# Ring of three tiles up to quad 60, sums for quads 73 to 76, and the change into block 1 by halves

## The chip, the cores and the metric

The kernel runs on one core of one Trainium2 chip. The metric is the device time of one execution in microseconds (us), lower is better. TensorE (PE) multiplies matrices, ScalarE (ACT) applies functions, VectorE (DVE) does elementwise work and reductions, GpSimd (POOL) small elementwise work, SyncE (SP) issues DMAs.

## What is computed

Attention with an additive score over 77 context tokens, and then an FFN with weights and activations rounded to FP4 by blocks of 16. The rows are 2 x 2048 with 512 features.

```
x = x + _L0_xattn_ref(_layernorm(x), mask, ctx, mask2, Ws, W, w, b, Wcw, bcw, Wcb, bcb)
x = x + _L0_ffn_ref(_layernorm(x), w_gate, w_up, w_down)

def _L0_xattn_ref(features, masks, textual_features, q_masks, Ws, W, w, b, Wcw, bcw, Wcb, bcb):
    txt_proj = einsum('btd,de->bte', textual_features, Ws)
    feat_proj = einsum('bfd,de->bfe', features, W)
    h = tanh(txt_proj[:, None, :, :] + feat_proj[:, :, None, :] + b)
    rho = einsum('bftd,d->bft', h, w[:, 0]) + (1.0 - q_masks)[:, None, :] * NEG
    att = softmax(rho, axis=-1)
    txt_h = einsum('bft,btd->bfd', att, textual_features)
    w_s = tanh(einsum('bfd,od->bfo', txt_h, Wcw) + bcw)
    b_s = tanh(einsum('bfd,od->bfo', txt_h, Wcb) + bcb)
    return w_s * features + b_s

def _L0_ffn_ref(x, w_gate, w_up, w_down):          # fp4_linear rounds x and w to FP4
    h = silu(fp4_linear(x, w_gate)) * fp4_linear(x, w_up)
    return fp4_linear(h, w_down)
```

## The kernel before

**Tanh and scores.** The 4096 rows are four blocks of 1024. For each block, tanh is taken of (features + text) for 77 tokens x 512 features. The work is cut into quads, 77 a block (QPB), numbered through all blocks: quad n is four rows of 1024 columns (128 features x 1024 rows of x, for four pairs of token and feature group). ACT makes a quad with four ACTIVATEs, features plus a bias column a token, into a place of a ring (`tanh_quad`, L628). PE scores it with 8 products of 512 columns into `rho` (`score_quad`, L809) and frees the place. Some quads are summed: DVE adds the bias column first (`sum_quad`, L985), into a room (`room_of`), and ACT then needs one ACTIVATE of 4096 columns (L623). `ring_pos` says which place a quad uses and `ring_prev` which quad it must wait for. In block 0 the ring has the two places of `hring` and a third, `HEAD_PLACE`: 4 is a part of `featT` that later blocks' features fill, 3 is `wd_room`, which the down weights fill later, None is no third place. Before: place 4 for quads up to 42, none for 43 and 44, place 3 for 45 to 60. The eight quads `FIRST_SUMS` are summed in `wd_room`, in the rounds `SUM_ROUNDS` of DVE.

**The head, block 0.** Beside the quads, PE turns and projects the rows of blocks 1 to 3 in twelve pairs of tiles: `turn_pair(w)` (L824) waits for `pair_normal` of GpSimd (L501) and writes the banks tr and dn, DVE copies them (`copy_pair`, L1120), PE projects (`project_pair`, L836, two halves), DVE copies the features out (`features_pair`, L1131). Pair w is tied to quad 8 + 9w/2. A DVE round w is: `copy_pair(w)`, a sum, `gate_up_weights(w + 1)` (rounding weights to FP4, with the statistics of two pairs in every other round), `features_pair(w - 1)`, a sum. Then DVE rounds the down weights, which SP transposes into `wd_room` after the last quad that used it (`LAST_IN_WD`).

**The change into block 1.** After quad 76, DVE adds the mask (`softmax_drain`, L1219), PE transposes the scores, DVE subtracts the maxima (`softmax_shift`), ACT takes the exponentials of both halves (L636), DVE makes the sums `garg` for both halves (`softmax_sums`), ACT takes the tanh `gates` (L655), DVE makes the factors and then tile 0 of the FFN (`rows_tile(0)`), which SP transposes for PE. ACT meanwhile makes the quads of block 1, of which PE scores seven (`PRE_QUADS`) before FFN tile 0.

**The stream.** From then on PE walks through 32 FFN tiles t of 7 pieces p: four gate and up pieces (L892) and three down pieces of the tile before (L906). `slots[t, p]` says how many quads it scores behind each piece, spread by the costs `G_COST` and `D_COST` between the ends of two blocks; `before[t, n]` counts quads up to a piece. ACT makes quads up to `before[t, n]` plus the ring's depth, then the silu of a piece (L661). DVE multiplies (`hidden`, L1309), rounds (`quantise_hidden`) and sums quads in between. Block k ends in tile `BASE[k] - 2`, that is 6, 14 and 22, `SOFTMAX_AT`, with its softmax there. The last quads stand in tile 22. Each engine runs its list in order and waits on semaphores.

## Time and profile before

| | us |
|---|---|
| median of 3 timed runs | 1537.94 |
| lowest, highest | 1537.92, 1540.9 |
| the profiled execution, its own time | 1539.24 |
| its span in the profile | 1537.4 |
| PE busy | 1432.1 (93%) |
| ACT busy | 1359.6 (88%) |
| DVE busy | 1157.2 (75%) |
| POOL busy | 248.7 (16%) |

Start times below are from the span's start. A row of the order of time gives the start of a group of like instructions, how long it lasts, engine and line, output and input tiles with sizes, how many (x), and in brackets how long the engine stood idle before it and what it waited for. "issue" there is a wait without a releaser in the profile. Two ACTIVATEs overlap by a little, so the difference of two starts is the cost of one.

### The profile page before, as it was taken

To read this page: it belongs to the slowest core of one execution; us is meant where nothing else is said; L and a number is where in the kernel's file an instruction comes from. 1 tells how busy PE (TensorE), PEld (TensorE's weight loads), DVE (VectorE), ACT (ScalarE), POOL (GpSimd) and SP (SyncE) were. 2 spreads that over 40 slices of the span, in tenths; PEclk is the share of its full clock that TensorE was granted. 3 is DMA by queue.
4 is the path that set the end of the run, shared out by engine and by line. 5 is a ranking of instruction groups with operands and counts; after the bars stand their busy time and mean duration, and the time that the engine had idled before them with its cause. 6 is when DMAs were issued, how large, how long until landed. Compare 5 with 4: busy or idle time off the path is not lost.

```text
span 1537.4 us, 24122 instructions
## 1 busy us (share of the span) xinstructions
PE 1432.1 (93%) x9752; PEld 647.7 (42%) x9752; DVE 1157.2 (75%) x1783; ACT 1359.6 (88%) x1249; POOL 248.7 (16%) x389
## 2 busy tenths in 40 slices
PE   7988889856999999999999999989999999999998
PEld 4444444411333333334444444434444444555564
DVE  4699997944586666759666776698877787898887
ACT  5999989999999999999999999999999999433321
POOL 0122222200111010111011111011101111312211
PEclk9999999988999999999999999999999999999999
DMA  5133332320011111201111111112111111123332
GB/s 159 42 83 83 83 82 75 95 65 8 8 26 41 40 27 41 40 15 40 41 40 40 41 33 37 36 40 40 40 41 41 40 41 40 40 59 73 80 69 62
DMA packets 181557, 77.91 MB, mean 51 GB/s; under 512 B 163627, under 2 KB 165675, under 8 KB 181445
## 3 DMA queue, kind: packets, MB, share of 16 engines
q1 hardware_dynamic: 180224, 75.00, 21.0%
q8 instruction: 76, 1.25, 0.3%
q10 hardware_dynamic: 1221, 1.36, 0.3%
q14 instruction: 36, 0.29, 0.1%
HBM read 27.85 MB, written 8.39 MB: 24 GB/s over the span
## 4 chain that ended last, share of the span: by engine, by line
PE 52%; ACT 27%; DVE 17%; issue 2%; DMA 1%; POOL 1%; SPq 0%; ACTq 0%; DVEq 0%; POOLq 0%
PE rho L809 19%; ACT hring L628 17%; PE dn L906 10%; PE gu1g L892 5%; PE gu0g L892 5%; PE gu1u L892 5%; PE gu0u L892 5%; ACT hring L623 4%; DVE featT L985 2%; ACT wd_room L628 2%; DVE work L1019 2%; ACT featT L623 1%; ACT featT L628 1%; DVE work L1040 1%; DVE work L1039 1%
## 5 line engine op out<-in xcount | busy, mean ns | idle before, releaser
L628 ACT ACTIVATE hring<-featT,bias 128x1024 f32<-128x1024 f32 x688 | 729.2, 1156 | 2.6 <-PE rho L809 2.5
L809 PE MATMUL rho<-hring,wslide 128*32 128x512 f32 x3776 | 459.0, 611 | 61.5 <-ACT hring L628 52.4
L809 PEld LDWEIGHTS rho<-hring,wslide 128*32 128x32 f32 x3776 | 105.5, 111 | 338.6 <-issue 191.7
L628 ACT ACTIVATE featT<-featT,bias 128x1024 f32<-128x1024 f32 x220 | 236.3, 1178 | 2.2 <-PE rho L809 2.2
L906 PE MATMUL dn<-wd_room,turned 128*128 128x512 f16 x1023 | 230.6, 380 | 0.2 <-DMA turned<-work 0.2
L490 POOL TENSOR_SCALAR split_t<-sm 128x32 f32<-128x32 f32 (+4 forms) x82 | 19.7, 240 | 1178.1 <-DVE sm L1008 1178.1
L623 ACT ACTIVATE hring<-featT 128x4096 f32<-128x4096 f32 x57 | 207.5, 3640 | 0.4 <-DVE featT L985 0.4
L985 DVE TENSOR_SCALAR featT<-featT,bias 128x1024 f32<-128x1024 f32 x256 | 175.5, 750 | 11.9 <-ACT hring L623 7.6
L1309 DVE TENSOR_TENSOR work<-sg,gu1u 128x352 f32<-128x352 f32 x64 | 33.3, 521 | 173.9 <-ACT sg L661 173.1
L906 PEld LDWEIGHTS dn<-wd_room,turned 128*128 128x128 f16 x1023 | 96.4, 98 | 145.2 <-issue 36.0
L809 PE MATMUL rho<-featT,wslide 128*32 128x512 f32 x1056 | 126.4, 596 | 5.4 <-ACT featT L628 3.1
L892 PE MATMUL gu1g<-wgu,turned 128*128 128x352 f16 x768 | 125.5, 313 | 4.1 <-DVE work L1309 3.9
L892 PE MATMUL gu0g<-wgu,turned 128*128 128x352 f16 x768 | 125.5, 313 | 2.3 <-DVE work L1309 1.9
L892 PE MATMUL gu0u<-wgu,turned 128*128 128x352 f16 x768 | 125.0, 313 | 0.0
L892 PE MATMUL gu1u<-wgu,turned 128*128 128x352 f16 x768 | 125.0, 313 | 0.0
L493 POOL TENSOR_TENSOR s_lo<-sm,s_hi 128x32 f16<-128x32 f32 (+4 forms) x82 | 111.0, 1353 | 6.4
L892 PEld LDWEIGHTS gu1g<-wgu,turned 128*128 128x128 f16 x768 | 71.8, 98 | 72.5 <-issue 28.5
L892 PEld LDWEIGHTS gu0g<-wgu,turned 128*128 128x128 f16 x768 | 71.8, 98 | 72.4 <-issue 26.8
L892 PEld LDWEIGHTS gu0u<-wgu,turned 128*128 128x128 f16 x768 | 75.1, 98 | 39.4
L892 PEld LDWEIGHTS gu1u<-wgu,turned 128*128 128x128 f16 x768 | 75.2, 98 | 39.3
L661 ACT ACTIVATE sg<-gu1g 128x352 f32<-128x352 f32 x64 | 30.5, 476 | 60.4 <-PE gu1u L892 60.4
L661 ACT ACTIVATE sg<-gu0g 128x352 f32<-128x352 f32 x64 | 30.5, 477 | 52.6 <-PE gu0u L892 52.5
(228 smaller groups left out, 1578.5 us busy)
## 6 DMA issues: line engine op xcount, KB each, us to landing
xt<-in_x SPq DMA_DIRECT2D x32, 256.0 KB, 2.8
out<-xt SPq DMA_DIRECT2D x32, 256.0 KB, 2.3
work<-in_x SPq DMA_DIRECT2D x8, 512.0 KB, 4.1
xt<-in_x SPq DMA_DIRECT2D x6, 512.0 KB, 4.3
xt<-in_L_ffn_w_gate SPq DMA_DIRECT2D x11, 256.0 KB, 2.7
xt<-in_L_ffn_w_up SPq DMA_DIRECT2D x11, 256.0 KB, 3.0
work<-in_L_ffn_w_down SPq DMA_DIRECT2D x2, 704.0 KB, 5.1
xt<-in_L_ffn_w_down SPq DMA_DIRECT2D x2, 704.0 KB, 4.1
```

Source lines behind the costliest of these rows:

```text
L490: small(pool.tensor_scalar(t, s, SPLIT, 1.0, ALU.mult, ALU.mult))
L493: pool.tensor_tensor(s_lo[:, 0:nb], s, s_hi[:, 0:nb], ALU.subtract).then_inc(split_ready, 1)
L623: act.activation(slot[s], rooms[room_of[n]], ACT.Tanh).then_inc(tanh_ready, GRP)
L628: act.activation(slot[s][:, g, :], featT[:, e, ROW0[k]:ROW0[k] + rows], ACT.Tanh, bias=bias[:, e, base + tok:base + tok + 1]).then_inc(tan ...
L661: act.activation(sg[:, n % 2, :], gu[n % 2][0][:, 0:GU_N], ACT.Silu, scale=1.0 / W_PRE).then_inc(sg_ready, 1)
L809: last = pe.matmul(rho[SLOTW * g:SLOTW * g + SLOTW, hf * 512:hf * 512 + 512], wslide[:, e, SLOTW - 1 - r:2 * SLOTW - 1 - r], slot[s][:, g, ...
L892: last = pe.matmul(ps[:, 0:GU_N], xqT[:, a, k, :], w[:, bb, k, n * GU_N:n * GU_N + GU_N], start=(k == 0 and i == 0), stop=(k == KC - 1 and ...
L906: last = pe.matmul(dn[:, :], hqT[:, a, c, :], wd[:, bb, c, :], start=(c == 0 and i == 0), stop=(c == NC - 1 and i == 2))
L985: dve.tensor_scalar(rooms[room_of[n]][:, g, :], featT[:, e, ROW0[k]:ROW0[k] + BLOCKS[k]], bias[:, e, tok:tok + 1], None, ALU.add).then_inc ...
L1019: ins = tt(a.rearrange("p (i q b) -> p i b q", **natural), src.rearrange("p (i b q) -> p i b q", **natural), r.rearrange("p (i b) -> p i b ...
L1039: step(tt(a, a, big, ALU.add))
L1309: signal(tt(h, sg[:, n % 2, :], gu[n % 2][1][:, 0:GU_N], ALU.mult), gu_drained[n % 2], 2 * t + n // 2 + 1)
```

## The change

- `PRE_QUADS` is 5 instead of 7.
- The third place in block 0 is place 4 up to quad 51 and place 3 for quads 52 to 60.
- A ninth first sum, quad 49, in DVE round 8. Four late sums, quads 73 to 76: 73 and 75 in a room of two pieces (`stage` and part of `turned`, two ACTIVATEs of 2048 columns), 74 and 76 in `work`. DVE makes the first behind the last down weights and the others behind the wait for their transposing; 75 waits for the tanh of 73, 76 for that of 74.
- Block 1 has 23 summed quads instead of 22, from its quad 7 on (before from 12).
- For even pairs w > 0, PE now does both halves of `project_pair(w - 1)` one quad earlier and `turn_pair(w)` behind them.
- The sums, gates and factors of the change into block 1 are made by halves of four tiles: half 0, tile 0, half 1.
- Block 1 ends in tile 6 after piece 4 instead of 2, and block 2 starts accordingly. DVE puts block 1's drain and shifts into the rounding of tile 6 and the sums behind it. ACT makes quads up to 156 before the exponentials.

```diff
-PRE_QUADS = 7
+PRE_QUADS = 5
-    HEAD_PLACE = [4] * 43 + [None] * 2 + [3] * 16 + [None] * (QPB - 61)
-    SUM_ROUNDS = (0, 2, 4, 6)
-    FIRST_SUMS = (13, 17, 22, 26, 31, 35, 40, 44)
+    HEAD_PLACE = [4] * 52 + [3] * 9 + [None] * (QPB - 61)
+    SUM_ROUNDS = (0, 2, 4, 6, 8)
+    FIRST_SUMS = (13, 17, 22, 26, 31, 35, 40, 44, 49)
+    LATE_SUMS = (73, 74, 75, 76)
...
+    ENDS = [(0, -1), (BASE[1] - 2, 4), *((b - 2, 2) for b in BASE[2:])]
...
-    SUMS = {1: range(12, QPB, 3), 2: [3, *range(11, QPB, 4)], 3: [2, 5, *range(11, QPB, 3)]}
+    WHOLE = {1: range(7, QPB - 3, 3), 2: [3, *range(11, QPB, 4)], 3: [2, 5, *range(11, QPB, 3)]}
...
@@ scalar, change into block 1 @@
             tanh_quad(issued, range(3, 4))
-            tanh_quad(issued + 1)
-            tanh_quad(issued + 2, range(0, 1))
-            softmax_gates(0)
-            tanh_quad(issued + 2, range(1, 4))
-            issued += 3
+            tanh_quad(issued + 1, range(0, 2))
+            half_gates(0, first_garg, first_gates)
+            tanh_quad(issued + 1, range(2, 4))
+            tanh_quad(issued + 2)
+            tanh_quad(issued + 3)
+            half_gates(1, garg_ready, gates_ready)
+            issued += 4
@@ scalar, SOFTMAX_AT @@
-                    if issued < QUADS:
+                    goal = 2 * QPB + 3 if SOFTMAX_AT[t] == 1 else min(issued + 1, QUADS)
+                    while issued < goal:
@@ tensor, quads of block 0 @@
                     at = 8 + 9 * w // 2
-                    if n == at and w < PAIRS:
+                    behind = w % 2 == 0 and w > 0
+                    if n == at and w < PAIRS and not behind:
                         turn_pair(w)
-                    if n == at + 1 and w > 0:
+                    if n == at + (0 if behind else 1) and w > 0:
                         project_pair(w - 1, 0)
-                    if n == at + 2 and w > 0:
+                    if n == at + (1 if behind else 2) and w > 0:
                         project_pair(w - 1, 1)
+                        if behind and w < PAIRS:
+                            turn_pair(w)
@@ vector, rounds @@
-                if w in SUM_ROUNDS:
+                if w in SUM_ROUNDS[:-1]:
                     sum_quad()
...
             down_weights(3)
+            sum_quad()
             dve.wait_ge(wd_turned, 16 * KC)
+            for _ in LATE_SUMS[1:]:
+                sum_quad()
@@ vector, new @@
+            def first_sums(hf, made):
+                part = slice(4 * hf, 4 * hf + 4)
+                e = rhoS[:, hf * 512:hf * 512 + 512].rearrange("p (t s) -> p t s", t=4)[:, :, 0:TOK]
+                t = prod.rearrange("p (t s) -> p t s", t=4)[:, :, 0:TOK]
+                dve.wait_ge(exp_ready, hf + 1)
+                step(dve.tensor_reduce(den[:, part], e, axis=AX_X, op=ALU.add))
+                step(dve.reciprocal(den[:, part], den[:, part]))
+                for u in range(2):
+                    step(tt(t, e, uv[:, 0, u, :].unsqueeze(1).broadcast_to([P, 4, TOK]), ALU.mult))
+                    step(dve.tensor_reduce(garg[:, u, part], t, axis=AX_X, op=ALU.add))
+                    ins = tt(garg[:, u, part], garg[:, u, part], den[:, part], ALU.mult)
...
+            def first_factors(hf, made):
...
+                dve.wait_ge(made, 2)
...
@@ vector, change into block 1 @@
-            softmax_sums(0)
-            softmax_factors(0)
+            first_sums(0, first_garg)
+            first_factors(0, first_gates)
             rows_tile(0)
+            first_sums(1, garg_ready)
+            first_factors(1, gates_ready)
+            first_results(1)
+            sum_quads(QPB + 4)
@@ vector, tile 6 @@
+                if begun == 1:
+                    rows_tile(t + 1)
+                    hidden(t, 2)
+                    hidden(t, 3)
...
+                    quantise_hidden(t, between=lambda: softmax_drain(1), midway=shifts)
+                    softmax_sums(1)
```

PE in block 0, from quads 15 and 16 on, before. `rho<-` rows are scores (x8 is a quad), `gu1g` and `gu1u` are the halves of `project_pair(1)`, `tr` and `dn` from `work` are `turn_pair(2)`:

```order
42 L809 MATMUL rho<-hring,wslide 32x512 x16
43 L809 MATMUL rho<-featT,wslide 32x512 x8
44 L824 MATMUL tr<-idf,work 128x128 x4
45 L824 MATMUL dn<-idf,work 128x128 x4
46 L809 MATMUL rho<-hring,wslide 32x512 x8
47 L836 MATMUL gu1g<-stage,turned 128x256 x8
48 L809 MATMUL rho<-hring,wslide 32x512 x8
49 L836 MATMUL gu1u<-stage,turned 128x256 x8
50 L809 MATMUL rho<-featT,wslide 32x512 x8
```

The same place now:

```order
42 L834 MATMUL rho<-hring,wslide 32x512 x16
43 L834 MATMUL rho<-featT,wslide 32x512 x8
44 L861 MATMUL gu1g<-stage,turned 128x256 x8
45 L834 MATMUL rho<-hring,wslide 32x512 x8
46 L861 MATMUL gu1u<-stage,turned 128x256 x8
47 L849 MATMUL tr<-idf,work 128x128 x4
48 L849 MATMUL dn<-idf,work 128x128 x4
49 L834 MATMUL rho<-hring,wslide 32x512 x8
50 L834 MATMUL rho<-featT,wslide 32x512 x8
```

The turning of pair 2 moved from behind quad 17 to behind both projection halves and quad 18.

ACT at the end of block 0, before (a row of 128x1024 is a fourth of a quad, `stage<-stage` are the exponentials, `sg` is the first silu of the stream):

```order
64 L628 ACTIVATE hring<-featT,bias 128x1024 x71
65 L636 ACTIVATE stage<-stage 128x4x77 x2
66 L628 ACTIVATE hring<-featT,bias 128x1024 x6
67 L655 ACTIVATE gates<-garg,bc 128x8 x2
68 L628 ACTIVATE hring<-featT,bias 128x1024 x23
69 L661 ACT_TABLE_LOAD
70 L661 ACTIVATE sg<-gu0g 128x352
```

And now:

```order
65 L638 ACTIVATE hring<-stage 128x2048
66 L638 ACTIVATE hring<-turned 128x2048
67 L638 ACTIVATE hring<-work 128x4096
68 L638 ACTIVATE hring<-stage 128x2048
69 L638 ACTIVATE hring<-turned 128x2048
70 L638 ACTIVATE hring<-work 128x4096
71 L644 ACTIVATE hring<-featT,bias 128x1024 x7
72 L652 ACTIVATE stage<-stage 128x4x77 x2
73 L644 ACTIVATE hring<-featT,bias 128x1024 x3
74 L711 ACTIVATE gates<-garg,bc 128x4 x2
75 L644 ACTIVATE hring<-featT,bias 128x1024 x10
76 L711 ACTIVATE gates<-garg,bc 128x4 x2
```

Quads 73 to 76 come from rooms, the gates stand in two pairs, and the second pair stands ten rows behind the first.

DVE at the change into block 1, before (the end of the sums of half 1, then the factors):

```order
378 L1252 TENSOR_REDUCE garg<-stage 128x4
379 L1253 TENSOR_TENSOR garg<-garg,den 128x4
380 L1251 TENSOR_TENSOR stage<-stage,uv 128x4x77
381 L1252 TENSOR_REDUCE garg<-stage 128x4
382 L1253 TENSOR_TENSOR garg<-garg,den 128x4
383 L1266 TENSOR_TENSOR beta<-gates,rstd 128x8
```

And now, from the end of tile 0's rounding:

```order
410 L1075 TENSOR_TENSOR xq<-work,s_lo 128x512
411 L1339 TENSOR_TENSOR beta<-beta,stat 128x4
412 L1340 TENSOR_TENSOR beta<-gates,beta 128x4
413 L1374 TENSOR_SCALAR xt<-xt,alpha,beta 128x512
414 L1312 TENSOR_REDUCE den<-stage 128x4
415 L1313 RECIPROCAL den<-den 128x4
416 L1315 TENSOR_TENSOR stage<-stage,uv 128x4x77
417 L1316 TENSOR_REDUCE garg<-stage 128x4
```

The sums of half 1 moved from ahead of the factors to behind tile 0.

## Rows read from the trace of the kernel before

**Rows 1.** Windows: busy PE, PEld, DVE, ACT, POOL (instructions), granted clock, DMA, GB/s

```profile
77.00:227.00 150.00, 132.51 (x872) 68.63 (x868) 143.14 (x231) 143.21 (x119) 40.45 (x48) 0.97 0.31 79
308.00:357.00 49.00, 29.71 (x204) 7.37 (x200) 20.74 (x23) 48.78 (x47) 3.63 (x4) 0.84 0.22 52
390.00:1314.00 924.00, 891.70 (x6423) 370.91 (x6420) 674.85 (x990) 920.77 (x798) 124.49 (x180) 1.00 0.17 36
```

**Rows 2.** Order of time, ACT in block 0: summed quads and waits

```profile
153.50 3.62 ACT L623 ACTIVATE hring<-wd_room 128x4096 f32<-128x4096 f32 x1 [0.40 <-DVE wd_room L985]
158.27 4.27 ACT L628 ACTIVATE featT<-featT,bias 128x1024 f32<-128x1024 f32 x4 [1.15 <-PE rho L809]
...
170.76 3.60 ACT L623 ACTIVATE featT<-wd_room 128x4096 f32<-128x4096 f32 x1
174.26 8.42 ACT L628 ACTIVATE hring<-featT,bias 128x1024 f32<-128x1024 f32 x8
...
192.03 3.62 ACT L623 ACTIVATE hring<-wd_room 128x4096 f32<-128x4096 f32 x1 [1.04 <-DVE wd_room L985]
196.67 4.27 ACT L628 ACTIVATE featT<-featT,bias 128x1024 f32<-128x1024 f32 x4 [1.02 <-PE rho L809]
...
212.32 3.62 ACT L623 ACTIVATE hring<-wd_room 128x4096 f32<-128x4096 f32 x1 [3.07 <-issue]
...
308.22 48.95 ACT L628 ACTIVATE hring<-featT,bias 128x1024 f32<-128x1024 f32 x47 [0.58 <-PE rho L809]
```

**Rows 3.** Order of time, PE around the turning of pair 2

```profile
100.39 1.92 PE L809 MATMUL rho<-featT,wslide 128*32 128x512 f32 x16 [0.37 <-ACT featT L623]
104.03 0.66 PE L824 MATMUL tr<-idf,work 128*128 128x128 f32 x4 [1.71 <-POOL work L501]
...
105.05 1.92 PE L809 MATMUL rho<-hring,wslide 128*32 128x512 f32 x16
106.90 3.72 PE L836 MATMUL gu1g<-stage,turned 128*128 128x256 f32 x16
110.55 1.92 PE L809 MATMUL rho<-hring,wslide 128*32 128x512 f32 x16
```

**Rows 4.** Order of time, DVE: copies of pairs 2 and 8, a sum, a wait

```profile
110.60 0.69 DVE L1120 COPY stage<-tr 128x512 f32<-128x512 f32 x1
...
189.17 2.74 DVE L985 TENSOR_SCALAR wd_room<-featT,bias 128x1024 f32<-128x1024 f32 x4
...
226.32 0.69 DVE L1120 COPY stage<-tr 128x512 f32<-128x512 f32 x1
...
268.98 0.69 DVE L1131 COPY featT<-gu1g 128x512 f32<-128x512 f32 x1 [8.17 <-PE gu1u L836]
```

**Rows 5.** Order of time, DVE and then ACT, the change into block 1

```profile
351.94 1.29 DVE L1219 TENSOR_SCALAR stage<-rho,negm 128x1024 f32<-128x1024 f32 x1 [20.45 <-PE rho L809]
...
360.79 0.47 DVE L1247 TENSOR_REDUCE den<-stage 128x4 f32<-128x308 f32 x1
...
364.71 0.17 DVE L1266 TENSOR_TENSOR beta<-gates,rstd 128x8 f32<-128x8 f32 x1 [0.79 <-ACT gates L655]
...
374.95 0.55 DVE L1303 TENSOR_SCALAR xt<-xt,alpha,beta 128x512 f32<-128x512 f32 x1
...
357.07 0.80 ACT L636 ACTIVATE stage<-stage 128x308 f32<-128x308 f32 x2
...
364.13 0.47 ACT L655 ACTIVATE gates<-garg,bc 128x8 f32<-128x8 f32 x2
364.51 23.99 ACT L628 ACTIVATE hring<-featT,bias 128x1024 f32<-128x1024 f32 x23
```

**Rows 6.** Order of time, block 1's softmax in tile 6: DVE, then ACT

```profile
698.57 0.17 DVE L1253 TENSOR_TENSOR garg<-garg,den 128x4 f32<-128x4 f32 x1
...
700.53 0.47 ACT L655 ACTIVATE gates<-garg,bc 128x8 f32<-128x8 f32 x2
```

**Rows 7.** Order of time, ACT: the last scores are drained

```profile
1316.33 1.11 ACT L640 ACTIVATE stage<-rho,negm 128x1024 f32<-128x1024 f32 x1 [1.70 <-PE rho L809]
```

91 lines of the change are left out of this document (66 added, 25 removed).

## The prediction

> **What bounds the kernel now.** Three views, in this order. The busy time by stretch [rows 1]: between 390 and 1314 us ScalarE (ACT) is busy for 920.77 of 924.00 us, TensorE (PE) for 891.70, VectorE (DVE) for 674.85. The reader is to see that ACT, which makes the tanh tiles that PE scores, has 3.2 us of room in the whole stretch. So whatever lets ACT enter it earlier, or takes work from it there, moves the end one for one, as long as PE and DVE keep up. The last scores are drained at 1316.33 [rows 7]; what follows is FFN work that the change leaves alone, so the tail keeps its length.
> The second view is ACT's order of time in block 0 [rows 2]. It waits six times between 150 and 310 us: 0.40 and 1.04 us for a sum by DVE, and 1.15, 1.02, 3.07 and 0.58 us for a ring place (the 3.07 us carries no releaser; quad 44 goes there into the place of quad 42). In the same region DVE is busy 143.14 of 150.00 us in 231 instructions [rows 1], with some 0.03 us between two of them: it never stands still, and what delays DVE there delays every later sum. The third view is the order of time around the change into block 1 [rows 5].
>
> The unit is read from ACT's rows. The 47 rows from 308.22 to the exponentials at 357.07 are quads 67 to 77 and three rows of quad 78 [rows 2, 5]: 48.85 / 47 = 1.039 us a row, 4.16 us a quad. A summed quad takes 174.26 - 170.76 = 3.50 us [rows 2], so a sum saves ACT 0.65 us. Quad 76 ends at 308.22 + 40 x 1.039 = 349.8; I call this E.
>
> **Part 1, the order of PE in the head.** For even pairs turn_pair now stands behind both halves of project_pair. For pair 2 before, PE took quad 17 at 100.39, waited 1.71 us for GpSimd, and turned from 104.03 to 105.05 [rows 3]. Now: quad 17 takes 1.86 us, to 102.25; a half projection takes 110.55 - 106.90 = 3.65 us, to 105.9; quad 18 to 107.8; the second half to 111.4; the turning, 1.02 us, to 112.45. DVE wanted the result at 110.60 [rows 4]. It now waits 1.9 us, and as it has no idle time, its chain of rounds runs 1.9 us later from there. For pairs 4 and 6 the same steps put the end of the turning at 148.7 and 187.2; DVE wants them at 151.1 and 189.6 with its delay, so 2.4 us are left and nothing is added. Behind DVE's wait stand the sums for quads 22 to 44, and ACT waits for those.
> ACT then runs so. Quad 31: its sum comes 1.9 us later than before, and it starts at 155.4 instead of 153.50. Quad 32: its wait of 1.15 us is gone, since PE no longer holds scores back behind GpSimd: 0.75 us late. Quad 40: ACT arrives at 192.03 - 1.04 + 0.75 = 191.7, the sum (189.17 + 2.74 + 1.9 [rows 4]) is there at 193.8: again 1.9 late. Quad 41: its 1.02 us is gone: 0.9 us late.
>
> **Part 2, three ring places up to quad 60.** Quad 44 goes to the third place, free since quad 41 is scored, so the 3.07 us goes: it starts at 196.67 + 0.9 + 3 x 4.16 = 210.05 instead of 212.32. What is late next is the new ninth sum, for quad 49: DVE copies pair 8 from 226.32 + 1.9 on (two copies of 0.69 us), then sums for 2.74 us, ready at 232.4 [rows 4]. ACT would be there at 210.05 + 3.50 + 4 x 4.16 = 230.2 and starts at 232.5; before, it was there at 232.7. So nearly all that the third place gives is spent waiting: 0.2 us is left, and 0.65 us by the sum itself. The sum's own 2.74 us on DVE is hidden, since DVE idled 8.17 us at 269 [rows 4]. From quad 61 on the ring has two places while the last pair is projected: two waits of about 0.5 us where there was one of 0.58, 0.4 us lost. At quad 67: **-0.45 us**.
>
> **Part 3, late sums for quads 73 to 76.** Two, in one piece of 4096 columns, save 0.65 us each. The other two come in two pieces of 2048. No row shows such a piece; between 1024 columns at 1.04 us and 4096 at 3.50 us a straight line gives 1.86, two of them 3.72, a saving of 0.43. The bounds for a quad are 4.16 and 3.50. In sum -2.2 us (bounds -1.3 and -2.6). The Trainium skill (ScalarE: Activation LUTs, What ACT_TABLE_LOAD costs) gives 186 ns + 0.833 ns a column, less 93 ns of overlap, without a bias pointer; by it two pieces would take 3.60 us and the sum would be 0.2 us better. By that rule 4096 columns take 3.50 us, and the trace agrees. The cover: sums 75 and 76 can only start when the tanh of 73 and 74 has emptied their room, and need 2.74 us against the 3.5 to 3.7 us of the quad between: 0.8 us to spare. DVE itself is free, it waited 20.45 us for the last scores [rows 5]. E becomes 349.8 - 0.45 - 2.2 = 347.2: **-2.6 us**.
>
> **Part 4, the change into block 1 by halves.** Half 0 is what PE's tile 0 needs, and it comes earlier: its gates stand 3 rows behind the exponentials instead of 6. But ACT's own order now asks for the gates of half 1 ten rows after those of half 0, 10.4 us. Between them DVE has to make the factors, tile 0, the betas and the row's result (364.71 to 374.95 + 0.55, 10.8 us), then the sums of half 1 (360.79 to 364.71 - 0.79, 3.1 us) [rows 5]: 13.9 us, with signals 14.15. **ACT waits 3.75 us** for garg. This wait did not exist, since the sums of both halves stood ahead of the gates. Behind it on ACT stand quads 82 and on, the whole stretch that has no room. Two more gate instructions cost 364.51 - 364.13 = 0.38 us. PE can start tile 0 some 12 us earlier than before, but then it waits for tanh tiles; its own work is not what bounds. In sum **+4.1 us**. GpSimd's share of tile 0 and SP's transposing keep their order.
>
> **Part 5, the stream.** One more sum in block 1: -0.65 us. PRE_QUADS 5 puts the same quads two earlier against the tiles; ACT's list is as long as before. Block 1's end moves two pieces on in tile 6. Before, garg was there at 698.57 + 0.16, 1.8 us ahead of ACT's gates at 700.53 [rows 6]. Now DVE ends the quantising first. From the end of quad 153's tanh ACT has three quads, the table and exponentials (2.1), a summed quad and a quad: 22.3 us. DVE has PE's score (1.9), the drain (1.3), a sum (2.7), two steps and both shifts with PE between them (5), the rest of the quantising (5.1) and twice 3.1 for garg: 22.3 us too. I take no wait (bounds 0 and 2.7, should one sum more fall ahead of garg).
>
> **Sum:** -2.6 + 4.1 - 0.65 = +0.85 us. On the profiled execution's 1539.24 us that is 1540.1; that execution lies 1.3 us above the median of the three timed runs, 1537.94. I forecast the median: **1538.8 us**. A measurement of this kernel can tell about 0.2% (3.1 us) from no change; this is within it.
>
> **Rivals.**
> R1, slower: DVE slips again. The decisive place is turn_pair of pairs 4 and 6, with 2.4 us to spare. Should PE run a half projection there at 1.2 GHz (the granted clock was 0.97 in the mean of 77 to 227 us, so for a part of it at the lower level [rows 1]), it takes 3.65 us more, the reserve is gone, and two slips of about 2 us reach quads 40 and 49: +4.9, 1542.8. For it: the same happens at pair 2 by my count. Against it: PE's waits for GpSimd, behind which it was slow, are what the new order removes.
> R2, faster: the wait at the second gates is small and DVE does not slip at pair 2. Then 3.75 and 1.9 us come off at most: -4.8, 1533.1. Against it: both are sums of rows on engines that have nothing else to do.
> R3: PE is at the lower clock (mean 0.84 between 308 and 357 us [rows 1]) when it scores quad 76; that takes 1.8 us more, DVE's chain to the exponentials is 0.4 us ahead of ACT, and ACT waits 1.4: +2.3, 1540.2. The Trainium skill (TensorE: Matmul & The Clock Gate, HAM oscillation) says that idle gaps put the array back to half speed; by it the two quads fewer ahead of tile 0 would make this likelier.
> R4: the stream's 3.2 us of waits [rows 1] go: -2.3, 1535.6; or tile 6 costs its 2.7: 1541.5.
> R5: the change doesn't do what it says, the late sums come late and save nothing: +3.05, 1541.0.
>
> **How the numbers follow.** Forecast as summed, 0.50, its own range 1537.3 to 1540.4; R1 0.15; R2 0.13; R3 0.07; R4 0.07; R5 0.08. Faster by over 3.1 us is R2: 0.13. Slower by over 3.1 us is R1, half of R5 and 0.01 of the forecast's tail: 0.20. Within: 0.67. The range 1535.0 to 1543.0 leaves out R2 and the outer part of R1, under 2 in 10.
>
> **What would show it.** Right: ACT waits 3 to 4.5 us before the second pair of gates and 2 to 2.5 us before quads 31, 40 and 49, for DVE's sums; it has no wait at quads 32, 41 and 44; DVE waits about 2 us for the turned pair 2; E is near 347. Wrong: under 1 us at the second gates, or ACT busy under 915 of 924 us in the stream, which would mean that PE or DVE has become what bounds.

## The result and the profile after

| | before | after |
|---|---|---|
| median | 1538.24 us (8 runs) | 1543.86 us (8 runs) |
| lowest, highest | 1537.81, 1540.9 | 1541.2, 1545.79 |
| ratio, 95% interval | | 1.0032 [1.0022, 1.0041] |
| the profiled execution | 1539.24 us | 1541.2 us |

The change makes the kernel 4.9 us slower (0.0032 of 1538). The forecast was 1538.8 us, in a range of 1535.0 to 1543.0; the measured median lies above it. The profiled execution after is the lowest of its eight. The same kernel, measured again in the run e1_again below (profiled at 1543.47 us), is nearer to the median, so the ledger has both.

The windows of the kernel after, which answer to [rows 1]: PE, PEld, DVE, ACT and POOL busy, granted clock, DMA, GB/s.

```profile
77.00:227.00 150.00, 136.95 (x904) 71.41 (x896) 141.28 (x229) 145.92 (x122) 42.36 (x48) 0.97 0.31 79
308.00:357.00 49.00, 30.51 (x212) 7.33 (x208) 31.96 (x45) 48.42 (x41) 3.67 (x4) 0.86 0.22 52
390.00:1314.00 924.00, 888.73 (x6392) 369.92 (x6394) 669.24 (x981) 919.00 (x795) 124.47 (x180) 1.00 0.17 36
```

ACT now stands still for 5.0 us of the 924 instead of 3.2, although it is still the engine that bounds. Where it stands, the order of time shows. ACT in block 0, answering to [rows 2]; "<-" names what ended the wait:

```profile
153.96 3.62 ACT L638 ACTIVATE hring<-wd_room 128x4096 f32<-128x4096 f32 x1 [1.99 <-DVE wd_room L1015]
...
192.28 3.62 ACT L638 ACTIVATE hring<-wd_room 128x4096 f32<-128x4096 f32 x1 [2.09 <-PE rho L834]
...
208.28 3.60 ACT L638 ACTIVATE featT<-wd_room 128x4096 f32<-128x4096 f32 x1
...
230.61 3.62 ACT L638 ACTIVATE hring<-wd_room 128x4096 f32<-128x4096 f32 x1 [2.10 <-PE rho L834]
...
284.71 16.74 ACT L644 ACTIVATE hring<-featT,bias 128x1024 f32<-128x1024 f32 x16 [0.58 <-PE rho L834]
...
302.03 29.22 ACT L644 ACTIVATE hring<-featT,bias 128x1024 f32<-128x1024 f32 x28 [0.58 <-PE rho L834]
...
338.94 1.93 ACT L638 ACTIVATE hring<-stage 128x2048 f32<-128x2048 f32 x1 [0.58 <-PE rho L834]
340.77 1.89 ACT L638 ACTIVATE hring<-turned 128x2048 f32<-128x2048 f32 x1
342.57 3.60 ACT L638 ACTIVATE hring<-work 128x4096 f32<-128x4096 f32 x1
```

Quads 31, 40 and 49 wait 2.0 to 2.1 us each; quad 44 (208.28) waits for nothing. At 192.28 and 230.61 the row names PE, but DVE finished the sum only then:

```profile
111.30 0.69 DVE L1150 COPY stage<-tr 128x512 f32<-128x512 f32 x1 [1.89 <-PE dn L849]
...
189.42 2.74 DVE L1015 TENSOR_SCALAR wd_room<-featT,bias 128x1024 f32<-128x1024 f32 x4
...
227.76 2.74 DVE L1015 TENSOR_SCALAR wd_room<-featT,bias 128x1024 f32<-128x1024 f32 x4
```

189.42 + 2.74 = 192.16, and ACT starts 0.12 us later; 227.76 + 2.74 = 230.50, and ACT starts 0.11 us later. The first row is DVE's wait for pair 2, 1.89 us. The change into block 1, ACT, answering to [rows 5]:

```profile
357.16 0.47 ACT L711 ACTIVATE gates<-garg,bc 128x4 f32<-128x4 f32 x2
...
371.71 0.49 ACT L711 ACTIVATE gates<-garg,bc 128x4 f32<-128x4 f32 x2 [3.68 <-DVE garg L1317]
```

And tile 6, where block 1 now ends: ACT, then PE, then DVE, and last PE's granted clock (the column behind the five engines).

```profile
685.98 3.62 ACT L638 ACTIVATE featT<-featT 128x4096 f32<-128x4096 f32 x1 [0.61 <-issue]
...
693.66 0.48 ACT L671 ACTIVATE gates<-garg,bc 128x8 f32<-128x8 f32 x2
...
696.76 4.27 ACT L644 ACTIVATE hring<-featT,bias 128x1024 f32<-128x1024 f32 x4 [0.49 <-PE rho L834]
...
670.68 1.92 PE L834 MATMUL rho<-hring,wslide 128*32 128x512 f32 x16 [2.23 <-ACT hring L644]
...
679.34 1.09 PE L908 MATMUL tr<-gat,stage 128*128 128x77 f32 x8 [3.19 <-DVE stage L1261]
680.26 3.73 PE L934 MATMUL dn<-wd_room,turned 128*128 128x512 f16 x9
683.93 1.93 PE L834 MATMUL rho<-featT,wslide 128*32 128x512 f32 x16
...
674.06 2.74 DVE L1015 TENSOR_SCALAR featT<-featT,bias 128x1024 f32<-128x1024 f32 x4
...
678.71 0.48 DVE L1261 TENSOR_TENSOR stage<-tr,mx 128x308 f32<-128x308 f32 x1
...
692.87 0.16 DVE L1286 TENSOR_TENSOR garg<-garg,den 128x4 f32<-128x4 f32 x1
...
680.00:684.00 4.00, 4.00 (x17) 1.44 (x20) 3.36 (x4) 3.98 (x5) 0.00 (x0) 0.57 0.00 0
```

Quad 154 is block 2's first and has `featT` as its ring place; the ring has three places here, so ACT's quad 157 (685.98) goes into the same one, and starts when 154's score (683.93 + 1.93) is done. PE comes to 154 late: it stands idle for 3.19 us until DVE's shift of half 0, and ahead of that shift DVE has made a sum of 2.74 us. Behind these 3.19 us PE goes to the lower of its two clocks (1.2 and 2.4 GHz): the mean granted between 680 and 684 us is 0.57, and the nine products take 3.73 us, where e5_shift below has 2.11 at a granted clock of 1.00. At full clock 154's score would have been done 1.6 us earlier, which is more than ACT's wait of 0.61 (an estimate from these rows). By it the wait at quad 157 needed both, the late shift and the fall of the clock behind it. The garg that the forecast looked at (692.87 + 0.16) is there 0.6 us ahead of the gates (693.66).

### The ledger

Time between the starts of two quads' first ACTIVATEs, read from ACT's order of time; the difference to the kernel before beside the forecast's step.

| stretch | before, us | after | e1_again | forecast |
|---|---|---|---|---|
| quads 13 to 61 | 201.85 | -1.59 | -1.59 | -0.85 |
| quads 61 to 67 | 25.62 | +0.71 | +2.34 | +0.4 |
| quads 67 to 77 (late sums) | 41.58 | -1.71 | -2.09 | -2.2 |
| quads 77 to 90 (change into block 1) | 57.04 | +4.12 | +4.15 | +4.1 |
| quads 90 to 186 (tile 6 in it) | 399.65 | +1.69 | +1.75 | -0.65 |
| quads 186 to 306 | 499.30 | +0.04 | -0.01 | 0 |
| sum | | +3.3 | +4.5 | +0.8 |

Quad 13 itself starts at 80.75 us before, 79.61 after and 80.58 in e1_again. No instruction of the change lies ahead of it but the order of its loads, and among all profiles below it lies between 79.4 and 81.4, so it is scatter and is kept out of the sums.

The forecast put the 0.65 us of block 1's added sum into the stream, and the table follows it. The trace has it in the row above: quads 77 to 89 hold two summed quads instead of one, quads 90 to 185 hold 28 in both kernels. Put where they act, the forecast's steps are +3.45 for quads 77 to 90 and 0 for quads 90 to 186. The measured +4.12 holds two small things that the forecast did not have: ACT makes four silus there instead of three (0.36 us) and waits 0.26 us at quad 87.

### The profile page after: what moved, and what is told of

It reads as the page before. It is cut to its first block, busy times and chain, and to the rows that moved or that the text cites. A ratio compares the mean times of both kernels' runs of the same rounds, so it can differ in the third digit from the quotient of the medians.

```text
span 1539.4 us, 24158 instructions
## 1 busy us (share of the span) xinstructions
PE 1433.3 (93%) x9752; PEld 647.8 (42%) x9752; DVE 1176.4 (76%) x1826; ACT 1356.9 (88%) x1235; POOL 251.3 (16%) x389
## 3 DMA queue, kind: packets, MB, share of 16 engines
q8 instruction: 76, 1.25, 0.3%
## 4 chain that ended last, share of the span: by engine, by line
PE 57%; ACT 25%; DVE 14%; issue 1%; DMA 1%; POOL 0%; SPq 0%; ACTq 0%; DVEq 0%; POOLq 0%
PE rho L834 21%; ACT hring L644 15%; PE dn L934 11%; PE gu0g L920 6%; PE gu0u L920 6%; PE gu1g L920 5%; PE gu1u L920 5%; ACT hring L638 5%; ACT featT L644 3%; DVE featT L1015 2%; DVE work L1049 1%; ACT featT L638 1%; DVE work L1069 1%; DVE work L1070 1%; DVE sm L1035 1%
## 5 line engine op out<-in xcount | busy, mean ns | idle before, releaser
L644 ACT ACTIVATE hring<-featT,bias 128x1024 f32<-128x1024 f32 x668 | 708.5, 1157 | 4.8 <-PE rho L834 4.7
L644 ACT ACTIVATE featT<-featT,bias 128x1024 f32<-128x1024 f32 x228 | 244.8, 1175 | 0.0
L638 ACT ACTIVATE hring<-featT 128x4096 f32<-128x4096 f32 x58 | 211.2, 3641 | 0.7 <-DVE featT L1015 0.4
L834 PE MATMUL rho<-featT,wslide 128*32 128x512 f32 x1104 | 132.0, 596 | 6.6 <-ACT featT L644 4.1
L505 POOL TENSOR_TENSOR s_lo<-sm,s_hi 128x32 f16<-128x32 f32 (+4 forms) x82 | 106.3, 1296 | 6.4
L1380 DVE TENSOR_TENSOR work<-sg,gu0u 128x352 f32<-128x352 f32 x64 | 33.3, 520 | 56.3 <-ACT sg L677 54.0
```

The lines of the kernel that those rows point to most:

```text
L505: pool.tensor_tensor(s_lo[:, 0:nb], s, s_hi[:, 0:nb], ALU.subtract).then_inc(split_ready, 1)
L638: act.activation(slot[s][:, at:at + count, :], piece, ACT.Tanh).then_inc(tanh_ready, count)
L644: act.activation(slot[s][:, g, :], featT[:, e, ROW0[k]:ROW0[k] + rows], ACT.Tanh, bias=bias[:, e, base + tok:base + tok + 1]).then_inc(tan ...
L834: last = pe.matmul(rho[SLOTW * g:SLOTW * g + SLOTW, hf * 512:hf * 512 + 512], wslide[:, e, SLOTW - 1 - r:2 * SLOTW - 1 - r], slot[s][:, g, ...
L1380: signal(tt(h, sg[:, n % 2, :], gu[n % 2][1][:, 0:GU_N], ALU.mult), gu_drained[n % 2], 2 * t + n // 2 + 1)
```

## The experiments

The jobs ran on different chips. So each kernel is judged by its ratio to the kernel before on the same chip, and a difference of two ratios is turned into microseconds by 1538.6. e1 to e4 ran together, e5 to e8, e10 to e12, e13 with e14, and e15 with e16.

### e1_again to e4_end: one part undone each

e1_again is the changed kernel, unaltered: 1543.54 us, 1.0036 [1.0024, 1.0049]. It is the reference for the others. A cost that comes and goes, its theory A, shows in its trace: 1.6 us between quads 61 and 67, at 290 to 305 us, mostly ahead of the stretch that was named. The median lies 2.5 us above the 1541 of theory B. The edits of the others:

```diff
@@ e2_gates: ACT makes quad 82 ahead of the second gates @@
             tanh_quad(issued + 3)
+            tanh_quad(issued + 4)
             half_gates(1, garg_ready, gates_ready)
-            issued += 4
+            issued += 5
@@ e3_order: PE turns every pair at its old place @@
-                    behind = w % 2 == 0 and w > 0
+                    behind = False
@@ e4_end: block 1 ends behind piece 2 again, its drain and shifts not inside the rounding @@
-    ENDS = [(0, -1), (BASE[1] - 2, 4), *((b - 2, 2) for b in BASE[2:])]
+    ENDS = [(0, -1), *((b - 2, 2) for b in BASE[1:])]
-                    goal = 2 * QPB + 3 if SOFTMAX_AT[t] == 1 else min(issued + 1, QUADS)
+                    goal = min(issued + 1, QUADS)
...
-                    hidden(t, 1, sums=begun is None or begun == 1)
-                if begun == 1:
+                    hidden(t, 1, sums=begun is None)
+                if False:
```

> The changed kernel, unaltered. Its profiled execution was 2.0 us longer than the one of before, while the medians of eight runs are 5.6 us apart (1541.2 to 1545.8 us against 1537.8 to 1540.9), so the trace at hand is of one of the shortest executions. Theory A (a second cost that comes and goes): another execution shows a wait or a stretch of PE at the lower clock that the first trace lacks, worth 2 to 4 us, most likely between 300 and 400 us, where PE idles between quads. Theory B (the first trace is typical, the rest is how the runs scatter): the same waits of ACT again, 2.0 before quads 31, 40 and 49 and 3.7 at the second gates, and a median within 1 us of 1541.

> ACT makes quad 82 ahead of the gates of half 1 instead of behind them: four rows, 4.16 us, more than the 3.68 us that it waited for garg. If that wait is a loss that the stream carries to the end, this kernel is 3.7 us faster than the changed one: about 1540.2 us, ratio to before 1.001. If PE or DVE is what bounds behind it, the wait goes and the time stays at 1543.9, ratio 1.003.

> The changed kernel with turn_pair at its old place ahead of the projections, for all pairs. Theory of the forecast: DVE no longer waits 1.9 us for pair 2, its sums come 1.9 us earlier, PE's waits for GpSimd come back (1.15 and 1.02 us on ACT before quads 32 and 41); quad 49 is then bound by its sum 1.9 us earlier, so the kernel is 1.5 to 2 us faster than the changed one, about 1542. Rival: PE's waits of up to 4 us put its clock down and the scores later; then it is as slow as the changed one or slower.

> The changed kernel with block 1's end at its old place, tile 6 behind piece 2, with DVE's and ACT's old order there. From quad 90 to quad 306 the changed kernel lost 1.7 us against before, where I had expected a gain of 0.65. If the new end costs that, this kernel is 1.5 to 2.5 us faster than the changed one, and quad 306 starts as far from quad 90 as before. If it is the other placing of quads against tiles (two quads fewer ahead of tile 0), the time is the same as the changed one.

| | median, us | ratio, 95% interval | against e1_again |
|---|---|---|---|
| e2_gates | 1538.92 | 1.0006 [0.9997, 1.0014] | -4.6 us |
| e3_order | 1543.9 | 1.0037 [1.0025, 1.005] | +0.2 |
| e4_end | 1540.76 | 1.002 [1.0011, 1.0029] | -2.5 |

e2: the wait of 3.7 us at the second gates is gone, and by the times one edit of the order of ACT takes back nearly all of the change's cost, 4.6 us. The trace has 3.3 of it, quads 77 to 90, since a new wait of 0.80 us for DVE's sum of quad 84 comes in; where the rest comes from the trace does not show. e4: quads 90 to 186 take 0.79 us less than before instead of 1.75 more. So the new end costs 2.5 us by the trace and 2.5 by the times (ratios whose intervals overlap a little). That the -0.79 is near the forecast's -0.65 is chance. No sum was added in this stretch; what makes it is one silu fewer on ACT (36 instead of 37, 0.36 us) and 0.37 us less of waiting (1.13 instead of 1.50). e3: the 1.9 us slip of DVE is gone (quad 49 starts 2.9 us earlier than before, from the same quad 13, instead of 0.9), but nothing of it arrives. In its trace part of it goes between quads 49 and 77, behind PE, and quads 90 to 306 cost 2.3 us more than in e1_again, 1.5 of them in the stretch with tile 6. That is one profile, so I don't rest on it; e8 below asks the question better.

ACT at quad 157 in e2_gates' profile, the slowest of its eleven executions, PE ahead of it, and two windows with the granted clock:

```profile
688.29 3.62 ACT L638 ACTIVATE featT<-featT 128x4096 f32<-128x4096 f32 x1 [3.77 <-issue]
...
669.83 3.51 PE L835 MATMUL rho<-hring,wslide 128*32 128x512 f32 x16 [2.23 <-ACT hring L644]
...
680.09 1.96 PE L909 MATMUL tr<-gat,stage 128*128 128x77 f32 x8 [3.21 <-DVE stage L1262]
681.85 4.04 PE L935 MATMUL dn<-wd_room,turned 128*128 128x512 f16 x9
...
670.00:673.00 3.00, 3.00 (x16) 0.42 (x12) 0.00 (x0) 3.00 (x4) 0.00 (x0) 0.50 0.00 0
680.00:684.00 4.00, 3.91 (x14) 2.54 (x15) 1.77 (x3) 3.97 (x5) 0.00 (x0) 0.50 0.00 0
```

A quad's score takes 3.51 us here and 1.92 in the kernel after, the transposing 1.96 instead of 1.09: PE is at the lower clock already ahead of DVE's shift and again behind it, and the wait is 3.77 instead of 0.61 us. Against e4, quads 90 to 186 cost 2.5 us in the kernel after, where PE fell to the lower clock once, behind the shift, and 5.7 here, where it fell twice.

All five profiles with this order of tile 6 (after, e1, e2, e3, e15) have PE idle for 3.1 to 3.2 us there and at the lower clock right behind it. In the twelve others PE idles 1.25 to 1.27 us at this place, and only e11 and e16 have the lower clock behind it.

e1_again also shows what the forecast's two waits of 0.5 us between quads 61 and 67 can become. ACT, then PE:

```profile
299.12 4.27 ACT L644 ACTIVATE hring<-featT,bias 128x1024 f32<-128x1024 f32 x4 [0.86 <-PE rho L834]
304.62 6.35 ACT L644 ACTIVATE hring<-featT,bias 128x1024 f32<-128x1024 f32 x6 [1.24 <-PE rho L834]
...
289.99 3.55 PE L834 MATMUL rho<-hring,wslide 128*32 128x512 f32 x16 [2.67 <-ACT hring L644]
```

and PE's row for the same quad in the kernel after:

```profile
289.03 1.92 PE L834 MATMUL rho<-hring,wslide 128*32 128x512 f32 x16 [2.67 <-ACT hring L644]
```

PE scores the quad at 289.99 in 3.55 us, after an idle time of 2.67 us; in the kernel after it takes 1.92 behind the same 2.67. That costs 1.6 us there. The granted clock was 0.50 between 290 and 293 us, against 1.00 between 289 and 292 us in the kernel after. The 16 profiles of changed kernels fall into two groups in this stretch: quads 61 to 67 take 2.1 to 2.4 us more than before in ten (e1 to e6, e11, e12, e14, e16), and 0.71 us more in the other six.

### e5_shift to e8_pair2: the mechanism at tile 6, and do the parts add

```diff
@@ e5_shift: the sum of quad 157 between the two shifts of tile 6 @@
-                                straight=straight, at=before[t, 4], between=between,
+                                straight=straight, at=None if t == 6 else before[t, 4], between=between,
...
                         softmax_shift(1, 0)
+                        sum_quads(before[t, 4])
                         softmax_shift(1, 1)
@@ e8_pair2, on top of e7_gates_end: pair 2 alone is turned at its old place @@
-                    behind = w % 2 == 0 and w > 0
+                    behind = w % 2 == 0 and w > 2
```

e6_both is e5_shift with e2's edit, e7_gates_end has the edits of e2 and e4.

> The changed kernel, but in tile 6 DVE makes the sum for quad 157 between the two shifts of block 1's end and not ahead of both, so PE gets the scores of half 0 about 2.8 us sooner. Theory A (quad 157 takes the ring place of quad 154, and PE comes to 154 late because it stands idle 3.2 us for the first shift): ACT's waits at quads 157 and 159 (0.6 and 0.5 us in the changed kernel's profile, up to 3.8 in a profile where PE was at the lower clock there) go, and the time falls by 2.4 to 2.9 us, to 1540.7 to 1541.3. Rival B (the loss in tile 6 is ACT's wait for the sums garg behind the exponentials, or the work of the end itself): nothing is gained, 1543.5 to 1544.

> The order of tile 6 of the run above, and also quad 82 on ACT ahead of the second gates of the change into block 1. Theory A: two separate causes, so the gains add: 4.6 us for the gates (1543.7 less 1538.9 of the runs with that edit alone) and 2.4 to 2.9 for tile 6, 1536.0 to 1537.0. Rival B: only one of them counts, because what ACT gains at the gates it stands waiting in tile 6: 1538.5 to 1539.5.

> Quad 82 ahead of the second gates, and block 1 ends in tile 6 behind piece 2 as in the kernel before. Theory A: additive, 1540.8 (end alone) less 3.7 (the wait at the second gates in the trace) is 1537.0; 1.5 us below the kernel before, with a head that is 1.6 to 2.6 us better and no loss in tile 6. Rival B: the gain at the gates is lost again in the stream, 1539 to 1540.5.

> As the run above, and PE turns pair 2 at its old place, ahead of the half projections; pairs 4, 6, 8 and 10 keep the new order. Theory A (the slip of DVE by 1.9 us comes from pair 2 alone, and quads 31, 40 and 49 wait for it): ACT's waits there fall from 2.0 to at most 0.3 us and quad 62 starts about 1.9 us earlier; up to 1.9 us of it reach the end, 1535.1 to 1536. Rival B (as in the run with all pairs at their old places, where 2.9 us gained at quad 49 had shrunk to 1.9 at quad 77): it is waited away again between quads 61 and 76 behind PE's scores, 1536.5 to 1537.5.

| | median, us | ratio, 95% interval |
|---|---|---|
| e5_shift | 1542.5 | 1.002 [1.0012, 1.0029] |
| e6_both | 1538.94 | 0.9998 [0.9989, 1.0007] |
| e7_gates_end | 1537.27 | 0.9987 [0.9978, 0.9996] |
| e8_pair2 | 1536.41 | 0.9979 [0.997, 0.9987] |

PE, ACT and the granted clock in tile 6 of e5_shift:

```profile
678.64 1.09 PE L908 MATMUL tr<-gat,stage 128*128 128x77 f32 x8 [1.25 <-DVE stage L1261]
679.57 2.11 PE L934 MATMUL dn<-wd_room,turned 128*128 128x512 f16 x9
681.60 1.92 PE L834 MATMUL rho<-featT,wslide 128*32 128x512 f32 x16
...
686.53 3.60 ACT L638 ACTIVATE featT<-featT 128x4096 f32<-128x4096 f32 x1
...
680.00:684.00 4.00, 4.00 (x32) 1.40 (x34) 3.90 (x6) 4.00 (x5) 0.00 (x0) 1.00 0.01 4
```

PE idles 1.25 instead of 3.19 us, the nine products take 2.11 instead of 3.73 since the clock stays full, quad 154 is scored 3.0 us ahead of ACT, and both waits (0.61 and 0.49) are gone. Quads 90 to 186 take 1.17 us less than in e1_again, the time 2.5 us less (ratios 1.0036 and 1.002, intervals that overlap a little). So DVE's order, PE's idle time and clock behind it, and the ring place are the mechanism for about half of the 2.5 us of the trace. How much of that half is the order and how much the clock no run shows, since they changed together. The rest, 1.4 us between e5_shift and e4_end, is for 0.75 us in waits of ACT (five of 0.25 to 0.45 us between 433 and 664 us, where e4 has two), and for the rest in rows that last a little longer. These waits stand ahead of tile 6, so the other spread of quads over the pieces, which the new end brings, is the likelier cause; no experiment took that apart.

By the ratios gates and end add: -4.6 and -2.5 us together would give 0.999, and e7 has 0.9987. Its rival B, that the gates' gain is lost again in the stream, falls. For gates and shift the times leave it open: together they would give 0.999 too, and e6 has 0.9998 [0.9989, 1.0007], 1.2 us less than e2 alone, and its median of 1538.94 us lies in its rival B's range. Its trace is on the side of theory A: no wait at quads 157 and 159, and quads 77 to 186 take 4.7 us less than in e1_again. Behind quad 186 nothing of it is lost.

By the times e8 gains another 1.2 us over e7, with intervals that overlap; the trace has 2.1 at quad 77. Without DVE's slip ACT waits 0.41 instead of 2.19 us at quad 31. But ACT still waits at quads 40 and 49. Its rows, and DVE's sums for these three:

```profile
153.63 3.62 ACT L638 ACTIVATE hring<-wd_room 128x4096 f32<-128x4096 f32 x1 [0.41 <-DVE wd_room L1016]
...
192.16 3.62 ACT L638 ACTIVATE hring<-wd_room 128x4096 f32<-128x4096 f32 x1 [2.30 <-DVE wd_room L1016]
...
230.66 3.62 ACT L638 ACTIVATE hring<-wd_room 128x4096 f32<-128x4096 f32 x1 [2.19 <-DVE wd_room L1016]
...
150.77 2.74 DVE L1016 TENSOR_SCALAR wd_room<-featT,bias 128x1024 f32<-128x1024 f32 x4
...
189.31 2.74 DVE L1016 TENSOR_SCALAR wd_room<-featT,bias 128x1024 f32<-128x1024 f32 x4
...
227.80 2.74 DVE L1016 TENSOR_SCALAR wd_room<-featT,bias 128x1024 f32<-128x1024 f32 x4
```

So my theory A for e8 was wrong about these two. The slip did reach them: counted from quad 13, quads 40 and 49 start 1.7 us earlier than in e7. But ACT's own arrival moved by as much. What makes the wait is the pace. DVE has no wait between 112 and 232 us, and its sums for quads 31, 40 and 49 stand 38.5 us apart (two rounds, 189.31 - 150.77 and 227.80 - 189.31). ACT needs 36.2 us for the nine quads between two of them (192.16 - 2.30 - 153.63), seven full and two summed. The missing 2.3 us are waited each time, wherever the first sum stands. Between quads 31 and 49 it is DVE and not ACT that sets the pace. Before, the sums for 31 and 40 also stood 38.5 us apart, and two waits for PE (1.15 and 1.02 us) hid a part of it.

### e10_late to e12_first: late sums, halves, block 1's first sum

All three on top of e8_pair2.

```diff
@@ e10_late @@
-    LATE_SUMS = (73, 74, 75, 76)
+    LATE_SUMS = ()
...
-            sum_quad()
             dve.wait_ge(wd_turned, 16 * KC)
@@ e11_whole: the change into block 1 as before @@
-PRE_QUADS = 5
+PRE_QUADS = 7
...
-            tanh_quad(issued + 1, range(0, 2))
-            half_gates(0, first_garg, first_gates)
-            tanh_quad(issued + 1, range(2, 4))
-            tanh_quad(issued + 2)
-            tanh_quad(issued + 3)
-            half_gates(1, garg_ready, gates_ready)
-            issued += 4
+            tanh_quad(issued + 1)
+            tanh_quad(issued + 2, range(0, 1))
+            softmax_gates(0)
+            tanh_quad(issued + 2, range(1, 4))
+            issued += 3
...
-            first_sums(0, first_garg)
-            first_factors(0, first_gates)
+            softmax_sums(0)
+            softmax_factors(0)
             rows_tile(0)
-            first_sums(1, garg_ready)
-            first_factors(1, gates_ready)
-            first_results(1)
@@ e12_first @@
-    WHOLE = {1: range(7, QPB - 3, 3), ...
+    WHOLE = {1: [8, *range(10, QPB - 3, 3)], ...
```

> The kernel of e8_pair2 without the late sums: quads 73 to 76 are made by four ACTIVATEs each. Theory A (the sums save what they save on ACT, two of 0.65 us and two of 0.5 us): quad 77 starts 2.2 us later, and the time is 1538.6. Rival B (a part is waited away, since PE at the lower clock scores quads 73 and 74 behind the shorter tanh): quad 77 1.6 us later, 1538.0.

> The kernel of e8_pair2, with the change into block 1 as in the kernel before (sums of both halves ahead of all gates, seven quads ahead of tile 0). Theory A (the halves give nothing, since ACT bounds the stream and PE's earlier tile 0 only waits; they cost two gate instructions, 0.38 us, and ACT's 0.8 us wait for the sum of quad 84 comes with them): 0.4 to 1.2 us less, 1535.2 to 1536.0. Rival B (PE's earlier tile 0 helps ACT's first quads of the stream): 0.5 to 2 us more, 1536.9 to 1538.4.

> The kernel of e8_pair2, with block 1's first sums at its quads 8 and 10 instead of 7 and 10. Theory A (ACT waits 0.81 us for DVE's sum of quad 84, which DVE makes only behind the factors of half 1): this wait goes and nothing comes in its place, 1535.6. Rival B (ACT then waits as long for a ring place or a silu): 1536.4, as before.

| | median, us | ratio, 95% interval | against e8_pair2 |
|---|---|---|---|
| e10_late | 1538.29 | 0.9999 [0.9991, 1.0008] | +3.1 us |
| e11_whole | 1536.41 | 0.9983 [0.9974, 0.9991] | +0.6 |
| e12_first | 1534.72 | 0.9972 [0.9962, 0.9983] | -1.1 |

The late sums are worth 1.8 us in the trace up to quad 77 and 3.1 in the times. e10's trace loses another 2.5 us between quads 77 and 90, where PE makes the last scores and the transposes of block 0 at the lower clock (1.96 and 1.91 us instead of 1.09 and 1.06) and ACT waits 1.24 us for the exponentials' input and 1.00 for a score. That is near to the forecast's R3, in a kernel without the late sums. The halves' worth is not settled. e11's interval overlaps e8's; but e11 has no wait for the sum of quad 84, and against e12, which has none either, it is 1.7 us slower on the same chip, with intervals that overlap. In e11's trace ACT gets from quad 13 to quad 90 in 1.4 us less than in e12, and gives it back to PE's scores at 555 us (1.32 us) and at quad 157 (1.94 us, PE at the lower clock). e12 takes away a wait of 0.81 us for the sum of quad 84, and its trace gains 0.93 us between quads 77 and 90; the times' 1.1 have intervals that overlap.

### e13_ninth and e14_later: does a wait for a sum count

On top of e12_first.

```diff
@@ e13_ninth: no sum for quad 49 @@
-    SUM_ROUNDS = (0, 2, 4, 6, 8)
-    FIRST_SUMS = (13, 17, 22, 26, 31, 35, 40, 44, 49)
+    SUM_ROUNDS = (0, 2, 4, 6)
+    FIRST_SUMS = (13, 17, 22, 26, 31, 35, 40, 44)
@@ e14_later: the same sums for quads that come one later @@
-    FIRST_SUMS = (13, 17, 22, 26, 31, 35, 40, 44, 49)
+    FIRST_SUMS = (13, 17, 22, 26, 31, 35, 41, 45, 50)
```

> The kernel of e12_first without the ninth first sum (quad 49 by four ACTIVATEs). Theory A (the ninth sum takes away what the third place gives: it saves ACT 0.65 us and makes it wait 2.27 us for DVE): quad 53 starts 1.6 us earlier, and 1.0 to 1.6 us of that reach quad 77; 0.9967, 1533.5. Rival B (what ACT gains at quad 49 it waits for PE's scores at quads 52 to 66, where two ring places are left and the pairs are projected): quad 77 starts at the same time, and the time is as that of e12_first, 1534.7, or 0.65 us more.

> The kernel of e12_first with the last three first sums for quads 41, 45 and 50 instead of 40, 44 and 49. Theory A (ACT only comes too early to sums that DVE makes when it can): the waits of 2.28 us at quads 40 and 49 go, quad 53 starts 2.3 us earlier and not 4.6, since quad 53's place in time is set by DVE's sum only through the last of them and ACT's three sums save the same; about 2 us reach quad 77; 1532.7. Rival B (ACT meets PE's scores instead, as after quad 61): at most 0.6 us, 1534.1 to 1534.7.

e13_ninth: 1535.54 us, 0.9968 [0.9957, 0.998]. e14_later: **1530.55 us, 0.9945 [0.9932, 0.9959]**, 8.5 us better than the kernel before. ACT in e14_later at quads 41, 45 and 50, all three summed:

```profile
192.98 3.60 ACT L638 ACTIVATE featT<-wd_room 128x4096 f32<-128x4096 f32 x1
...
208.96 3.60 ACT L638 ACTIVATE hring<-wd_room 128x4096 f32<-128x4096 f32 x1
...
229.77 3.62 ACT L638 ACTIVATE featT<-wd_room 128x4096 f32<-128x4096 f32 x1 [0.58 <-DVE wd_room L1016]
```

DVE's sums are made at the same time as ever; ACT simply has another quad to make in between, 4.16 us. The waits of 2.28 and 2.27 us shrink to 0 and 0.58, quad 61 starts 4.1 us earlier than in e12 counted from quad 13, and quad 77 4.8. The times say 4.2. I had expected about 2 us, since I took the two waits for one; each is an own loss, 2.3 us by which DVE's 38.5 us are longer than ACT's nine quads. One more quad in between gives DVE 4.16 us once, nearly enough for both. e13's median gains 0.6 us only. Its profiled execution, the lowest (1531.5 us, granted clock 0.993, the others 0.986 to 0.990), gains 2.0 us up to quad 61, more than theory A asked, and keeps it; another 1.6 us came because PE was at full clock between quads 61 and 67 there and not in e12's profile. Where the other executions lose it again I have not seen, so this run leaves open how much of the gain is there as a rule.

### e15_later_alone and e16_later2

e15_later_alone is the changed kernel with e14's line alone. e16_later2 is e14_later with (13, 17, 22, 26, 32, 36, 41, 45, 51).

> The changed kernel with one edit: the last three first sums for quads 41, 45 and 50 instead of 40, 44 and 49. Pair 2 keeps its new place, so DVE's sums stand 1.9 us later than in e14_later. Theory A (what ACT stands waiting for at quads 31, 40 and 49 is lost to the end one for one): the waits of 2.1 us at quads 40 and 49 go, quad 53 starts 3.0 to 3.6 us earlier relative to quad 13, and the time falls by as much, 1540.4 to 1541.0, ratio 1.0013 to 1.0017. Rival B (the gates' wait of 3.7 us and tile 6 take it back, since DVE and PE and not ACT set the time there): under 1 us, 1.0030.

> The kernel of e14_later (1530.5 us, 0.9945) with the first sums for quads 32, 36 and 51 instead of 31, 35 and 50. Theory A: the two waits that are left, 0.37 us at quad 31 and 0.58 us at quad 50, go, and the time falls by 0.5 to 0.95 us, 1529.6 to 1530.0. Rival B (ACT then meets PE's scores or the ring in the same place): no change, 1530.5, or more if a score is late.

e15: 1539.03 us, 1.0005 [0.9996, 1.0014], 4.8 us less than e1_again. One line makes the change a draw; gates and tile 6 take nothing of it back. Up to quad 61 its trace gains 3.6 us, the most that theory A gave. Up to quad 77 it gains 3.8 over e1_again and 2.6 over the profile after: 1.6 us of the first is PE's clock between quads 61 and 67, and a new wait at quad 74 takes 1.4 and 1.0 back. ACT shows the three places that are left, DVE's late sum of quad 74, the gates and quad 157:

```profile
333.03 3.62 ACT L638 ACTIVATE hring<-work 128x4096 f32<-128x4096 f32 x1 [1.55 <-DVE work L1015]
...
369.30 0.48 ACT L711 ACTIVATE gates<-garg,bc 128x4 f32<-128x4 f32 x2 [3.68 <-DVE garg L1317]
...
683.59 3.62 ACT L638 ACTIVATE featT<-featT 128x4096 f32<-128x4096 f32 x1 [0.65 <-issue]
```

e16: 1531.41 us, 0.9952 [0.9939, 0.9964], no different from e14. Its two waits for sums are gone, but its profile has 1.95 us at quad 157 where e14 has 0.26, with PE's twelve products ahead of quad 154's score at 4.44 us instead of 2.75. The gain of up to 0.95 us is too small to be told beside that.

## Why the prediction was wrong

Part 1 was right as to the slip and the waits. DVE waited 1.89 us for pair 2 (forecast 1.9), and quads 31, 40 and 49 waited 2.0 to 2.1 us (forecast 1.9 later, 2.0 to 2.5 us of wait), with none at quads 32, 41 and 44. Pairs 4 and 6 did not slip, so R1 did not come. The size of it was a little off: DVE reached the sums for quads 40 and 49 0.5 to 0.8 us sooner than I had worked out, counted from quad 13, and the stretch to quad 61 gave 1.59 us instead of 0.85. What the forecast did not say is that these waits come back each round because DVE's two rounds are longer than ACT's nine quads; e8 and e14 show it.

Part 2 was right in that ACT spends the third place's gain waiting at quad 49. e14 shows that the wait was the point: it could be had back by one quad. The third place alone has no number. e9_places was to have the old places under the edits of e8 and gave no time: in the kernel, place 3 is the room of the first sums and may only be used behind the tanh of the last of them, quad 49 by now, so with place 3 from quad 45 on ACT waits for itself. So the old places cannot go with the ninth sum. The term that was mis-sized is "two waits of about 0.5 us where there was one of 0.58, 0.4 us lost". It measured 0.7 us in one profile and 2.3 in the other, because PE scored there at the lower clock. R3 had that mechanism, but at quad 76; in both profiles of the changed kernel that place was as forecast, and it happened at quad 62.

Part 3 was right in kind: -1.71 and -2.09 us against -2.2. The pieces of 2048 columns took 340.77 - 338.94 = 1.83 and 342.57 - 340.77 = 1.80 us where I had 1.86 from a straight line; the Trainium skill's price (ScalarE: Activation LUTs, What ACT_TABLE_LOAD costs), 186 ns + 0.833 ns a column less 93 ns, gives 1.80 and was the better one. What was missing is 0.58 us at quad 75 in the profile after, a score by PE at the lower clock.

Part 4 was right in its wait: 3.68 us against 3.75. R2 falls with it. That the whole stretch came out at +4.12 against +4.1 is in part luck: the added sum's 0.65 us, which the forecast booked in the stream, is saved here, and a fourth silu and a wait of 0.26 us made up for it.

**Part 5 is the step that failed.** "I take no wait (bounds 0 and 2.7 ...)" and "-0.65" for the stream came to +1.7: the new end costs 2.5 us (e4), and e5 shows the mechanism of 1.2 of them. The count compared ACT's gates with DVE's garg, 22.3 against 22.3 us, and on that it was right, there was no wait at the gates. But ACT has two more quads to make between its exponentials and its gates, and the first of them needs a ring place. I counted DVE's and ACT's chains through tile 6 and not PE's: PE waits for the shift of half 0, behind a sum; only then come the transposes, a down piece and quad 154, and ACT's quad 157 waits for 154's place. PE's clock fell behind its idle time too, which no term had for tile 6. The other 1.4 us stay open, for the greater part in waits and rows ahead of tile 6. The bound of 2.7 was for another mechanism. R4 gave it as "or tile 6 costs its 2.7", inside a share of 0.07; its 1541.5 us are 3.6 above before and were left out where the forecast added up "slower by over 3.1".

So of the 3.7 us between the forecast's sum and e1_again's ledger, 2.4 are tile 6 and the stream, 1.9 are quads 61 to 67, and 0.7 the other way are quads 13 to 61. The range was too narrow as well: its upper end held either R1 or tile 6, not two such terms at once. And PE's lower clock stands in three places that the sum had at full clock: quad 62, quad 75 and tile 6.
